# A deformable layer's sampling weights, handled in blocks of eight image rows instead of four

## What is computed

```python
x = x + L0(_gn(x), ...)      # two grouped binary 3x3 convolutions with batch normalisation
x = x + L1(_gn(x), ...)      # deformable convolution

# L1, for each position (h, w), group g of 8 channels (G = 8), tap k of 9:
value = xf @ vp_w.T + vp_b
om = depthwise3x3(x) @ om_w.T + om_b          # per group and tap: dy, dx, mask
py = h + base_y[k] + off_y;  px = w + base_x[k] + off_x
sampled = bilinear(value, py, px)             # zero outside the image
out = einsum('nhwgk,nhwgkc->nhwgc', mask, sampled) @ op_w.T
```

## Time and profile before

| | us |
|---|---|
| median of 3 runs | 3049.57 |
| lowest, highest | 3048.11, 3061.09 |
| profiled execution, its own time | 3050.65 |
| its span | 3048.9 |
| TensorE, matmuls busy | 2751.8 (90%) |
| TensorE, weight loads busy (beside them) | 2210.7 (73%) |
| VectorE, ScalarE, GpSimd busy | 2103.1, 2130.7, 1911.7 |
| line 1268, matmuls busy, idle before them | 1085.8, 117.9 |
| DMA queues 1 and 10, share of 16 engines | 54.8%, 9.5% |

### The profile page before, as it was taken

One profiled execution on the slowest core, in us unless ns is written; L12 is line 12 of the kernel. 1 busy time (PEld: TensorE's weight loads), 2 busy tenths in 40 slices (PEclk: granted clock), 3 DMA queues, 4 the chain that ended last, 5 costly groups with the idle time before them and its releaser, 6 DMA issues. The chain is left out here.

```text
span 3048.9 us, 116091 instructions
## 1 busy us (share of the span) xinstructions
PE 2751.8 (90%) x47624; PEld 2210.7 (73%) x47624; DVE 2103.1 (69%) x3108; ACT 2130.7 (70%) x4385; POOL 1911.7 (63%) x1451
## 2 busy tenths in 40 slices
PE   5888859994799999999998999999999999999998
PEld 3555536773587878778787787787887877777886
DVE  4454433334888697978788787969687888868763
ACT  2333336552887878888888787877888888778883
POOL 2000000001888888888888888888888888787883
PEclk9999979997899999999999999999999999999999
DMA  4443469994567666666666676766666767667564
GB/s 107 106 116 95 127 148 262 266 250 139 153 185 203 194 201 195 196 190 197 196 193 198 188 204 179 204 195 192 196 192 188 201 198 198 194 184 202 172 179 142
DMA packets 465563, 558.31 MB, mean 183 GB/s; under 512 B 173520, under 2 KB 417744, under 8 KB 465104
## 3 DMA queue, kind: packets, MB, share of 16 engines
q1 hardware_dynamic: 346832, 460.00, 54.8%
q10 hardware_dynamic: 118272, 91.76, 9.5%
HBM read 351.36 MB, written 200.19 MB: 181 GB/s over the span
## 5 line engine op out<-in xcount | busy, mean ns | idle before, releaser
L1268 PE MATMUL acc_p<-abuf,vbd 128*32 128x102 f32 (+7 forms) x27648 | 1085.8, 333 | 117.9 <-DMA abuf<-weight_scratch 112.9
L1268 PEld LDWEIGHTS acc_p<-abuf,vbd 128*32 128x32 f32 (+1 forms) x27648 | 874.0, 144 | 331.1 <-DMA abuf<-weight_scratch 132.0
L1104 ACT ACTIVATE dwt<-xp,wts 128x224 f32<-128x224 f32 x2016 | 799.7, 481 | 107.1 <-ACT wst L1127 101.8
L975 DVE TENSOR_TENSOR pr<-mh_p,ht 128x864 f32<-128x864 f32 x672 | 669.1, 1051 | 23.2
L243 PE MATMUL cv<-cin,wb 128*64 128x392 bf16 x6912 | 602.6, 338 | 26.0 <-ACT cin L222 26.0
L1247 PE MATMUL win_p<-pr,smat 128*128 128x160 f32 x4032 | 610.3, 306 | 9.8 <-POOL pr L1061 8.7
L1247 PEld LDWEIGHTS win_p<-pr,smat 128*128 128x128 f32 x4032 | 555.6, 191 | 30.8 <-POOL pr L1061 8.8
L243 PEld LDWEIGHTS cv<-cin,wb 128*64 128x64 bf16 x6912 | 410.2, 112 | 212.4 <-ACT cin L222 26.2
L1044 POOL TENSOR_TENSOR dwt<-dwt 128x896 f32<-128x896 f32 x224 | 512.3, 2287 | 4.7 <-ACT dwt L1104 4.7
L1058 POOL TENSOR_TENSOR pr<-pr 128x576 f32<-128x576 f32 x224 | 316.9, 1415 | 282.6 <-DVE pr L975 282.6
L1189 PE MATMUL om_p<-wts,omin 64*64 64x216 f32 x3584 | 377.7, 350 | 2.4 <-issue 2.4
(11 more groups left out here) (132 smaller groups left out, 2716.1 us busy)
## 6 DMA issues: line engine op xcount, KB each, us to landing
abuf<-weight_scratch SPq DMA_DIRECT2D x1568, 120.0 KB, 2.7
weight_scratch<-wst ACTq DMA_DIRECT2D x224, 400.0 KB, 3.6
xt<-x SPq DMA_DIRECT2D x128, 392.0 KB, 7.4
rows_scratch<-vsb SPq DMA_DIRECT2D x224, 128.0 KB, 3.2
vbd<-rows_scratch SPq DMA_DIRECT2D x896, 32.0 KB, 2.8
x_scratch<-xt SPq DMA_DIRECT2D x64, 392.0 KB, 6.8
y<-x SPq DMA_DIRECT2D x64, 392.0 KB, 4.1
x3h<-x_scratch SPq DMA_DIRECT2D x64, 392.0 KB, 4.4
```

Of the source, the lines that this page charges most:

```text
L975: dve.tensor_tensor(pr[:, j % 2, slots, :, :, :].rearrange("p k e x z -> p e k (x z)"), mh[:, a, :, :].rearrange("p (k x) z -> p k (x z)", ...
L1104: ins = act.activation(dwt[:, j % 2, k, :].rearrange("p (r w) -> p r w", w=W), image[:, r:r + BR, k % 3:k % 3 + W], ACT.Identity, scale=dw ...
L1268: mm = pe.matmul(acc_p[32 * (2 * s + b):32 * (2 * s + b) + 32, 0:TN].rearrange("p (k w) -> p k w", w=W)[:, k0:k1 + 1, x0:x1], vbd[0:K, 1 - ...
```

## The change

Weights are handled in blocks D of two tiles (8 rows).

- `windows` still makes one tile. `copy_weights` puts it in its half of a single `wst`; after the odd tile one write of both follows. An image column's elements are then PC = 80 floats apart.
- `abuf` is single but in two halves by columns with a semaphore each: half 0 takes four of the seven reads, half 1 three. The read of a half waits until `apply` of that half of the block before is done.
- `apply(i, j, half)` works on two tiles but one column range: in even steps half 0 (34 columns wide) of the block of tiles t-4 and t-3, in odd steps half 1 (26 wide) of the same block. A matmul covers up to five output rows instead of four. `copy_acc` copies both tiles of a block, in odd steps. The output of a tile is projected in step t+5 instead of t+2 (LAG = 5).
- Values are made two tiles ahead instead of four.
- The sums of the next pair move from one in each of steps 0 to 7 to `SUM_AT`, and loads and stores move with them. ScalarE's loop over the pairs is written out. Some operands of `products`, `merge` and `windows` stand in another order, with the same shapes.

```diff
-PC = BR * RT * 2
+PC = 2 * BR * RT * 2
+BAND = CT * PC
...
-        wst = sb("wst", [LANES, 2, GS, BAND])
-        abuf = sb("abuf", [128, 2, S, QC * PC])
+        wst = sb("wst", [LANES, GS, BAND])
+        abuf = sb("abuf", [128, S, QC * PC])
...
+        LAG = 5
-        LOAD_AT = {2: (1, 2), 4: (1, 3), 9: (2, 0), 12: (2, 1)}
+        LOAD_AT = {3: (1, 2), 6: (1, 3), 10: (2, 0), 13: (2, 1)}
+        SUM_AT = {0: (0,), 1: (1,), 2: (2,), 3: (3,), 5: (4,), 6: (5,), 7: (6, 7)}
-        STORE_AT = {6: (0, 0), 9: (0, 1), 13: (0, 2), 2: (1, 3)}
+        STORE_AT = {9: (0, 0), 12: (0, 1), 2: (1, 2), 5: (1, 3)}
+        READS = (4, 3)
...
+                def read_weights(i, j, half):
+                    D = (NT * i + j) // 2
+                    sp.wait_ge(w_out, 16 * (D + 1))
+                    wait(sp, amat_ok, 2 * (D - 1) + half + 1)
...
-                    read_weights(i, j)
+                    n = near(i, j, -3 if j % 2 else -2, first, last)
+                    if n:
+                        read_weights(*n, j % 2)
...
-                        if j < HALVES:
-                            sum_half(i + 1, j)
+                        for h in SUM_AT.get(j, ()):
+                            sum_half(i + 1, h)
...
                 def copy_weights(i, j):
-                    u = j % 2
-                    wait(act, w_out[u], 16 * turn(i, j))
-                    act.wait_ge(win_ok, NT * i + j + 1)
+                    t, u = NT * i + j, j % 2
+                    if u == 0:
+                        wait(act, w_out, 16 * (t // 2))
+                    act.wait_ge(win_ok, t + 1)
...
-                def apply(i, j):
+                def apply(i, j, half):
...
+                    qb, K, x0, x1 = ((0, 128, 0, 34), (1, 96, 30, W))[half]
+                    rows = range(max(0, y0 - 2), min(H, y0 + 2 * BR + 2))
                     for yq in rows:
-                        k0, k1 = max(0, yq - y0 - 2), min(BR - 1, yq - y0 + 2)
+                        k0, k1 = max(0, yq - y0 - 2), min(2 * BR - 1, yq - y0 + 2)
...
-                    n = near(i, j, -2, first, last)
+                    n = near(i, j, -5 if j % 2 else -4, first, last)
                     if n:
-                        apply(*n)
+                        apply(*n, j % 2)
                     windows(i, j)
```

More of the change, by code:

```diff
@@ L823, in phase @@
         def phase(i, j):
[L825 removed]
+            return NT * i + j + 3
         with nc.Block() as block:
@@ L904, in _ @@
                         step(i, j, i == 0, i == pairs - 1)
-                store_piece(pairs - 1, PIECES - 1)
+                for j, half in ((NT - 2, 0), (NT - 2, 1)):
+                    read_weights(pairs - 1, j, half)
+                for k in range(2, PIECES):
+                    store_piece(pairs - 1, k)
                 for k in range(PIECES):
@@ L1013, in _ @@
                 read_misc(0, group=0)
-                for j in range(4):
+                for j in range(2):
                     read_misc(j + 1, value=(0, j))
@@ L1026, in _ @@
                     step(pairs - 1, j, False, True)
-                for j in range(2):
-                    read_misc(N + j + 5, output=(pairs - 1, NT + j - 2))
+                for j in range(LAG):
+                    read_misc(N + j + 3, output=(pairs - 1, NT + j - LAG))
             @block.gpsimd
@@ L1149, in step @@
                         hats(*n)
-                    n = near(i, j, -2, first, last)
-                    if n:
+                    n = near(i, j, -LAG, first, last)
+                    if n and j % 2:
                         copy_acc(*n)
                     copy_weights(i, j)
-                    write_weights(i, j)
+                    if j % 2:
+                        write_weights(i, j)
                     n = near(i, j, 5, first, last)
@@ L1163, in _ @@
                 act.wait_ge(lines_in, 2 * 16)
-                for j in range(NT):
-                    step(0, j, True, False)
-                with act.Fori(1, pairs - 1) as i:
+                for i in range(pairs):
                     for j in range(NT):
-                        step(i, j, False, False)
-                for j in range(NT):
-                    step(pairs - 1, j, False, True)
-                for j in range(2):
-                    copy_acc(pairs - 1, NT + j - 2)
+                        step(i, j, i == 0, i == pairs - 1)
+                for j in (NT - 4, NT - 2):
+                    copy_acc(pairs - 1, j)
             @block.tensor
@@ new lines, in apply @@
+                        for s in range(S):
+                            for b in range(2):
+                                seen = abuf[0:K, s, :]
+                                at = (QB * qb + x0 - 32 * qb + 2) * PC + 4 * BR * (y0 + k0 - yq + 2) + 2 * k0 + b
+                                mov = bass.AP(seen.tensor, seen.offset + at, [seen.ap[0], [4 * BR + 2, n], [PC, x1 - x0]])
+                                mm = pe.matmul(
+                                    acc_p[32 * (2 * s + b):32 * (2 * s + b) + 32, 0:2 * TN].rearrange("p (k w) -> p k w", w=W)[:, k0:k1 + 1, x0:x1],
+                                    vbd[0:K, 1 - s, qb, yq // BR % VSLOT, :, :, 2 * (yq % BR) + b].rearrange("p g c -> p (g c)"),
+                                    mov, start=yq == rows[0] and qb == 0, stop=yq == rows[-1] and qb == 1,
+                                    skip_group_check=True)
@@ L1290, in _ @@
                         step(i, j, i == 0, i == pairs - 1)
-                for j in range(2):
-                    apply(pairs - 1, NT + j - 2)
-                    offsets_and_misc(N + j + 5, output=(pairs - 1, NT + j - 2))
+                for j in range(LAG):
+                    if j < 4:
+                        apply(pairs - 1, NT - 4 + j // 2 * 2, j % 2)
+                    offsets_and_misc(N + j + 3, output=(pairs - 1, NT + j - LAG))
         flag_far(nc, far, flag, misc)
```

109 lines of the change are left out of this document (45 added, 64 removed).

## The result

| | before | after |
|---|---|---|
| median of four runs each, us | 3048.84 | 2996.63 |
| lowest, highest | 3039.29, 3061.09 | 2996.41, 2998.01 |
| profiled execution, its own time and span | 3050.65, 3048.9 | 2998.01, 2996.1 |

The account below looks back on a forecast made before the run. The prediction took TensorE to bound the deformable layer, its only sizeable hole being the weights' read into abuf. It summed 3050.65 - 112.9 + 33 - 3.4 + 11.7 = 2979 us, range 2935 to 3045.

Parts of the forecast that it names:

- Part 1: Apply over two tiles, half the columns a step: fewer matmuls but the same columns, saving 0 us.
- Part 2: Apply's matmuls read elements 320 bytes apart instead of 160: taken as 0, outer bound 10% (109 us) either way.
- Part 3: Writing and reading the weights in fewer, larger transfers with more slack: apply's waits for abuf go, -112.9 us.
- Part 4: VectorE's moved sums: step 7 takes 14.57 us, misc of step 9 waits, +33 us; bounds +56, another +15.
- Part 5: ScalarE's fewer copies and writes, and reversed slots on VectorE and GpSimd: nothing.
- Part 6: Layer's start and end, with values two ahead and output five behind: start -3.4 us, end +11.7 us.
- Step 7 costs nothing: Rival: VectorE is far enough ahead that its longer step 7 adds no wait; 2946 us, chance 15%.
- Reads partly late: Rival: loads going out just ahead of the write bring back half the abuf waits; 3035 us, chance 13%.
- Fewer matmuls: Rival: weight loads are apply's hidden limit, so 271 us goes off TensorE; about 2819 us, chance 4%.
- Slower by spacing: Rival: apply's columns cost more with elements 320 bytes apart; 10.9 us for each per cent, 3088 at 10%; chance 9%.

Follow-up runs that it names:

- e6_elements_160_bytes: The changed kernel with apply reading neighbouring columns' elements 160 bytes apart as before (wrong elements), all else in place: 3008.13 us.
- e4_two_rows_a_matmul: The changed kernel with at most two output rows in a matmul of apply, 41984 instead of 20480 matmuls for the same columns: 3263.43 us.
- e2_thin_sums: The changed kernel with all eight sums of the next pair on 8 of 392 columns, most of sums and statistics left out: 2896.43 us.
- e8_thin_depthwise_add: The changed kernel with GpSimd's second depthwise add on 8 of 224 columns (wrong depthwise result), VectorE untouched: 2896.35 us, ratio 0.9493 to the kernel before.
- e9_two_sums_early: The changed kernel with single sums per step, two of eight moved to steps 12 and 13 of the pair before, none in steps 2 and 3: 2947.46 us.
- e5_one_sum_a_step: The changed kernel with one sum in each of steps 0 to 7 and the last piece's load in step 5: 2968.65 us, ratio 0.9723 to the kernel before.

## Why the prediction was right, and where it was not

The time came out 18 us above the forecast. That is closer than the working deserved: two terms were off by 52 and 67 us, in opposite directions. Term by term, in us:

| part | forecast | measured | from |
|---|---|---|---|
| 1, 2: apply | 0 | -52.4 | busy, 1085.8 to 1033.4 |
| 3: reads | -112.9 | -112.0 | waits, 112.9 to 0.9 |
| 4: VectorE and GpSimd | +33 | about +100 | see below |
| 6: start | -3.4 | -0.5 | windows of step 4 |
| 6: end | +11.7 | +12.5 | last windows to last project |

The terms add up to -52.4, and the span fell by 52.8; the agreement is better than the "about" in the fourth row warrants.

**Part 1 holds.** Fewer matmuls were worth nothing at the old distance, as `e6_elements_160_bytes` shows with the forecast's own 5.58 us. At the new distance they may be worth something: there a further instruction cost 2.7 to 3.0 ns (`e4_two_rows_a_matmul`), which for the 7168 that fell away would be, as an estimate, 19 to 22 of the 52 us; no run has the old matmuls at the new distance. The Trainium skill (TensorE: Matmul & The Clock Gate, "Wait — 56ns, not 53.3ns?") has 2.5 ns; that run's 2.7 to 3.0 come near it at 320 bytes, and `e6_elements_160_bytes` shows nothing of it at 160.

**Part 2 failed in its size.** "I take 0", with 10% either way as the bound: with the new distance apply was 5% cheaper. The bounds held it, and the reason given for an effect (a shared read limit) fits the runs, though none shows what is shared; but nothing in the profile of before could tell the sign. The run at 256 bytes shows how little a rule by width would have been worth: 160, 256 and 320 bytes give 1093.7, 1191.6 and 1033.4 us. The Trainium skill (SBUF — State Buffer, "Door 1: The DMA port swizzle") had been read as saying that nothing changes, since each element is in a 16-byte line of its own at either distance. These three numbers are against that reading.

**Part 3 holds**, with its mechanism. The reads of a half now take SyncE 1.5 to 1.8 us to issue (2.4 reckoned) and land in 4.1 where 2.7 at most had been reckoned; the slack of 13.6 us covered it. The write of 800 KB needs 5.1 us instead of 3.6. Nothing of this is seen by TensorE.

**Part 4 failed in its size.** The place was right (misc of step 9, behind GpSimd's depthwise), step 7 too (14.89 against 14.57). The step that failed is "copy_om follows copy_om in 9.57 us (1935.62 to 1945.19), which is TensorE's own pace, so VectorE keeps its phase". 9.57 was one interval in one pair. Over pairs 3 to 15 of the kernel before it is 9.7 to 10.1 in steps 0 to 4. After the change it is 9.8 to 10.0 in steps 0 to 3, while TensorE, with apply cheaper, wants 9.86 and 8.76 in turn, 9.3 in the mean: what part 2 gained, VectorE could not follow. (Not all of the hole comes from that: with apply at its old price, in `e6_elements_160_bytes`, 61.4 us stand before line 1191.) Two rows of the kernel before had it in the open (VectorE, ninth pair, steps 3 and 4), had I compared them with each other:

```profile
1936.59 1.50 DVE L965 TENSOR_TENSOR mh_p<-oms,ht 128x864 f32<-128x864 f32 x1
...
1946.17 1.82 DVE L965 TENSOR_TENSOR mh_p<-oms,ht 128x864 f32<-128x864 f32 x1
```

As long as TensorE stood still for its reads in some steps, VectorE caught up there. With the reads in time the phase grows: copy_om starts 0.97, 1.11, 2.17, 2.70 and 3.47 us into steps 0 to 4 of the changed kernel. Step 4 has no sum and resets it, but step 7 is entered at 2.57, not at 0.91, and step 8 at 8.38, not at 6.5. What it meets on GpSimd sets the pace: mask_hats lasts 1.8 us when it meets line 1052, up to 3.0 when it meets line 1050 (2.57 and 2.94 are the means of steps 5 and 9). From the end of windows to the next apply it takes 0.7, 0.5, 1.0, 0.3, 1.9 and 2.5 us longer in steps 3, 4, 5, 7, 8 and 9 than in undisturbed ones, together 6.9 us a pair or some 100 us in 15 pairs; the list of waits has 88.5 of it in two rows, and part of the rest is in offset rows that are spread out (line 1196 was busy for 377.7 us before, 387.9 after). The upper bounds of the part, 56 and 15, left it out. That the sums on VectorE make most of the hole `e2_thin_sums` shows, and that the turns with GpSimd set VectorE's pace `e8_thin_depthwise_add`; each took 100 us off the time, the second in part by GpSimd's own shorter work. So the prediction's 33 us had the right last link (GpSimd's depthwise ahead of misc) in step 9 alone, and four further steps wait for the same thing.

**Part 5 holds**: no wait on ScalarE's copies stands in the list but 1.6 us. **Part 6**, the end, from windows to the last project (TensorE's timeline, to be compared with the earlier trace rows):

```profile
2960.19 2.71 PE L1254 MATMUL win_p<-pr,smat 128*128 128x160 f32 x18
...
2963.36 5.25 PE L1277 MATMUL acc_p<-abuf,vbd 128*32 128x34 f32 x96
...
2975.49 4.89 PE L1277 MATMUL acc_p<-abuf,vbd 128*32 128x34 f32 x80 [0.89 <-DMA abuf<-weight_scratch]
...
2986.91 0.78 PE L1203 MATMUL misc<-accs,wts 64*64 64x112 f32 x8 [0.81 <-DVE y L988]
```

2987.69 - 2960.19 is 27.5 us, 26.7 reckoned. The start gained next to nothing, as windows of step 2 came 3.5 us earlier (800.45 us instead of 803.95) but windows of step 4 only 0.5 us (822.82 us instead of 823.33): the slower steps ruled again sooner than reckoned.

**The rivals.** *Step 7 costs nothing* is refuted by the waits of steps 8 and 9. *Reads partly late* isn't seen at all. *Fewer matmuls* were to take 271 us off apply; it lost 52, and none of them without the new distance. *Slower by spacing* had the right place and mechanism, and the wrong sign.

## What to carry to other kernels

When a wait of the bounding engine goes, the engines that had caught up in it lose the same time: compare their pace, as a mean over many steps and not from one interval, with the new pace of the bounding engine. An operation that shows two durations at the same shape is a sign of another engine in its way, and one that shows the same duration in every step may be waiting in every step: its price alone is read where the other engines are idle. Moving two operations to where the engine had room was worth some 20 us here (`e9_two_sums_early` against `e5_one_sum_a_step`), with nothing made smaller. How far apart a matmul's elements stand is a parameter to be measured; it has no direction that could be reckoned.

## What the runs showed of the hardware

- VectorE's operations with two operands in SBUF (sums, mask_hats) and GpSimd's additions exclude each other for whole instructions: 8 columns took 1.47 and 1.19 us, mask_hats 1.05 alone and 1.8 to 3.0 otherwise, a sum's two operations 0.61 and 0.63 alone and 1.03 and 1.7 otherwise. The products (line 981) and copy_om, which have one operand in PSUM, take 1.05 and 1.07 us in the mean. The Trainium skill states just this (SBUF — State Buffer, "Who interferes with whom"): with two SBUF inputs a VectorE instruction contends with a GpSimd instruction that reads SBUF, and the second to issue blocks until the first has finished. The trace agrees in both cases; the prediction should have weighed it.
- Four matmuls side by side on 32 columns each of the array, with elements 160, 256 and 320 bytes apart, took 1093.7, 1191.6 and 1033.4 us for the same columns; at 256 bytes ScalarE's taps took 590 ns instead of 488 as well. What the engines share there no run shows.
- With 41984 instead of 20480 instructions in apply, TensorE stood 203 us on nothing that the profile shows, and the mean granted clock was 0.948 instead of 0.970.
